# One image moved from the preparation into the first batch, the scan of the expert weights spread out, the router and the first feed-forward tokens rearranged

## The reference, cut to what matters

```python
# x: (4, 256, 48, 48) float32
x = x + conv(_ln_c(x))              # LayerNorm over the 256 channels at each pixel, then:
#   k    = relu(conv7x7_dilation2(ln, w1) + b1)            256 -> 128 channels
#   attn = softmax(relu(batchnorm(conv1x1(k, w2) + b2)))   49 weights for each pixel
#   out  = sum over the 49 taps p of shift_p(ln) * attn[p]
t = tokens(x)                       # (4, 2304, 256)
t = t + ffn(_ln_t(t))
#   logits = mean over an image's tokens @ Wr + br;  softmax, capacity scale, softmax, top 2 of 8 experts
#   h = gelu(xf @ W1[e] + b1[e]);  y = h @ W2[e] + b2[e];  weighted sum of the two experts
#   LayerNorm(out + x) * gamma + beta
```

## Time and profile before

| what | value |
|---|---|
| time of 3 runs: lowest, median, highest | 972.19, 973.37, 975.27 us |
| the profiled execution's own time | 967.95 us |
| its span, first to last instruction | 966.2 us |
| PE busy | 905.5 us, 94% |
| DVE, ACT, POOL busy | 698.6, 528.8, 143.4 us |

### The profile page before, as it was taken

One profiled execution on the slowest core, in us unless ns is written; L12 is line 12 of the kernel. 1 busy time (PEld: TensorE's weight loads), 2 busy tenths in 40 slices (PEclk: granted clock), 3 DMA queues, 4 the chain that ended last, 5 costly groups with the idle time before them and its releaser, 6 DMA issues. The chain is left out here.

```text
span 966.2 us, 19549 instructions
## 1 busy us (share of the span) xinstructions
PE 905.5 (94%) x7659; PEld 752.6 (78%) x7659; DVE 698.6 (72%) x1825; ACT 528.8 (55%) x981; POOL 143.4 (15%) x164
## 2 busy tenths in 40 slices
PE   2887999999999999899999948999999999999997
PEld 2776888888888888798999935777777777777776
DVE  4798566477658649745779867778877887788767
ACT  4797343443345221034445629677776878687751
POOL 1100010000010100200123220212121121212122
PEclk9899999999999999899999969999999999999999
DMA  9721311123200154620568663543364245423211
GB/s 220 206 73 50 99 50 51 51 75 79 64 26 26 40 164 123 193 50 2 148 170 224 152 165 77 142 105 66 85 162 100 51 99 154 93 64 85 67 34 50
DMA packets 134826, 95.01 MB, mean 98 GB/s; under 512 B 63579, under 2 KB 129516, under 8 KB 134636
## 3 DMA queue, kind: packets, MB, share of 16 engines
q1 hardware_dynamic: 134734, 93.77, 38.0%
HBM read 54.91 MB, written 29.40 MB: 87 GB/s over the span
## 5 line engine op out<-in xcount | busy, mean ns | idle before, releaser
L1335 PE MATMUL pM<-V,U 128*128 128x264 f16 (+3 forms) x2352 | 291.3, 281 | 0.0
L1335 PEld LDWEIGHTS pM<-V,U 128*128 128x128 f16 x2352 | 228.9, 98 | 43.1
L1876 ACT ACTIVATE gf<-pH,b1c,sc 128x384 f32<-128x384 f32 x192 | 127.7, 669 | 82.8 <-issue 67.2
L2169 PE MATMUL pH<-V,w1h 128*128 128x384 f16 x768 | 157.7, 328 | 4.4 <-ACT gf L1876 2.4
L2183 PE MATMUL pY<-w2h,gh 128*128 128x256 f16 x576 | 157.0, 273 | 0.3 <-DVE w2l L2028 0.3
L2183 PE MATMUL pY<-w2h,gl 128*128 128x256 f16 x576 | 157.0, 273 | 0.0
L2183 PE MATMUL pY<-w2l,gh 128*128 128x256 f16 x576 | 157.0, 273 | 0.0
L2036 DVE SCALAR_TENSOR_TENSOR gl<-gf,sc,gh 128x384 f16<-128x384 f32 x192 | 112.1, 620 | 48.9 <-ACT gh L1867 48.9
L2169 PEld LDWEIGHTS pH<-V,w1h 128*128 128x128 f16 x768 | 74.9, 98 | 54.1 <-ACT gf L1876 4.8
L1867 ACT ACTIVATE gh<-gf,sc 128x384 f16<-128x384 f32 x192 | 115.5, 616 | 0.0
L789 ACT CAST V<-pV 128x336 f16<-128x336 f32 x96 | 42.0, 437 | 132.1 <-PE pV L1306 132.1
(11 more groups left out here) (253 smaller groups left out, 1357.5 us busy)
## 6 DMA issues: line engine op xcount, KB each, us to landing
xa<-in_xt SPq DMA_DIRECT2D x16, 576.0 KB, 6.5
xs_scratch<-xs SPq DMA_DIRECT2D x16, 576.0 KB, 4.3
V<-t_scratch SPq DMA_DIRECT2D x24, 384.0 KB, 3.8
out<-o SPq DMA_DIRECT2D x23, 384.0 KB, 2.9
xs<-in_ew SPq DMA_DIRECT2D x16, 512.0 KB, 4.4
U<-xs_scratch SPq DMA_DIRECT2D x16, 480.0 KB, 4.7
V<-in_w1g SPq DMA_DIRECT2D x6, 784.0 KB, 8.8
w1r<-in_ew SPq DMA_DIRECT2D x8, 512.0 KB, 4.1
```

The source lines that it names most:

```text
L1335: return nc.tensor.matmul(out[:, :, first:end], U[:, k, hi_u, piece, :], V[:, b % 2, hi_v, k, c, :, first + TILES * d:end + TILES * d], st ...
L1876: nc.scalar.activation(gf[:, (JB * m + j) % GBUFS, :], pH[:, (JB * m + j) % HBUFS, 0:CN], ACT.Gelu, bias=b1c[:, j // FB, j % FB:j % FB + 1 ...
L2169: last = nc.tensor.matmul(pH[:, (JB * m + j) % HBUFS, 0:CN], w[:, k, c, f * P:(f + 1) * P], xT[:, s, x, c, :], start=(i == 0), stop=(i == ...
```

## The change

Five edits, each with its core in the diff.

- The preparation ends with image 3 in place of image 4. The first batch prepares five images (4 to 8), with tables of its own, and its `turn_v` run at points 2 to 13 in place of 0 to 11 (`TURNS_FROM`). At the start `tap_scale(0)` stands behind the first two of the six `bn_stats` of `ln(0)` in place of behind all of it.
- `UNITS_SLOT` spreads the 17 units over ten points.
- `BY_PE` becomes images 14 and 15: image 15 is summed by `sum_tokens`, `accumulate(15)` is gone, and `accumulate(13)` moves ahead of `statistics(14)`. `take_low` and `turn` of the two early chunks move behind the loop.
- The router: the factor 1/2304 goes into the router's weights ahead of the loop, one operation of the capacity scale goes, the constants `ones` and `mhalf3` are set in the first block, each weight load is issued as soon as its own expert's number is read, and ACT normalises and splits chunk 2 ahead of the first `gelus`, not behind.
- `HBUFS` goes from 3 to 5; two unused banks are given up for it.

```diff
-LN_SLOT = {0: 1, 3: 2, 6: 3, 10: 4}
-SPLIT_SLOT = {2: 1, 5: 2, 8: 3, 13: 4}
+LN_SLOT = [{0: 0, 2: 1, 5: 2, 8: 3, 11: 4}] + [{0: 1, 3: 2, 6: 3, 10: 4}] * (B - 1)
+NORM_SLOT = [{0: 0, 3: 1, 6: 2, 9: 3, 12: 4}] + [{1: 1, 4: 2, 7: 3, 11: 4}] * (B - 1)
+SPLIT_SLOT = [{1: 0, 4: 1, 7: 2, 10: 3, 13: 4}] + [{2: 1, 5: 2, 8: 3, 13: 4}] * (B - 1)
+TURNS_FROM = [2] + [0] * (B - 1)
...
-STAGES, UNITS_SLOT = 3, {1: 1, 2: 2, 3: 2, 4: 2, 5: 2, 6: 2, 7: 3, 8: 3}
+STAGES, UNITS_SLOT = 3, {1: 1, 2: 2, 3: 2, 4: 2, 5: 2, 6: 2, 7: 2, 8: 1, 9: 1, 10: 2}
...
-ADDED, BY_PE = 1, IMGS - 2
+ADDED, BY_PE = 1, (IMGS - 2, IMGS - 1)
...
-                if n - CHUNKS_AT - 2 in range(EARLY_CHUNKS):
-                    tokens.turn(sp, 0, n - CHUNKS_AT - 2)
+            tokens.turn(sp, 0, 0)
             store_stats(B - 1)
+            tokens.turn(sp, 0, 1)
...
             spread_mags(0)
-            ln(0)
+            ln_stats(0, third(0))
             tap_scale(0)
+            ln(0, range(NT // 3, NT))
             ln(1)
...
-                    m = V_TURNS * BI * (b + 1) + 2 * k
-                    turns = b < B - 1 and k < V_SLOTS
+                    m = V_TURNS * BI * (b + 1) + 2 * (k - TURNS_FROM[b])
+                    turns = b < B - 1 and 0 <= k - TURNS_FROM[b] < V_SLOTS
...
+            nc.vector.tensor_scalar(wrs[:, :, :], wrs[:, :, :], 1.0 / SB, None, ALU.mult).then_inc(wr_scaled, 1)
             for n in range(IMGS):
                 if 1 <= n <= BI:
                     normalise(B - 1, n - 1)
+                if n == IMGS - 2:
+                    accumulate(n - 1)
                 statistics(n)
...
-                if ADDED * BI < n < IMGS - 1:
+                if ADDED * BI < n < IMGS - 2:
                     accumulate(n - 1)
-                if n - CHUNKS_AT - 2 in range(EARLY_CHUNKS):
-                    tokens.take_low(dve, 0, n - CHUNKS_AT - 2)
-            accumulate(IMGS - 1)
+            for m in range(EARLY_CHUNKS):
+                tokens.take_low(dve, 0, m)
             take_stats(B - 1)
...
-            nc.vector.tensor_scalar(mean[:, :], mean[:, :], 1.0 / SB, None, ALU.mult).then_inc(mean_step, 1)
...
-            sum_tokens(BY_PE)
+            sum_tokens(BY_PE[0])
+            sum_added(B - 1)
             turn_stats(B - 1)
-            sum_added(B - 1)
+            sum_tokens(BY_PE[1])
             sum_shifts(B - 1)
...
-HBUFS, GBUFS = 3, JB
+HBUFS, GBUFS = 5, JB
...
-            nc.gpsimd.memset(ones[:, :], 1.0).then_inc(c_set, 1)
-            nc.gpsimd.memset(mhalf[:, :], -0.5).then_inc(c_set, 1)
-            pool.wait_ge(c_set, 2)
...
+            normalise(0, EARLY_CHUNKS)
             nc.scalar.activation(rc[:, 7:8], rc[:, 4:5], ACT.Gelu)
             split_w1(0)
+            take_x(0, EARLY_CHUNKS)
             act.wait_ge(bias_step, 1)
             gelus(0, 0)
-            normalise(0, 2)
-            take_x(0, 2)
...
-            do(nc.vector.tensor_scalar(r[:, 5, :], pY[0:B, 1, 0:EXPERTS], float(SB), None, ALU.mult))
-            do(nc.vector.reciprocal(r[:, 5, :], r[:, 5, :]))
-            do(nc.vector.tensor_scalar(r[:, 5, :], r[:, 5, :], CAPACITY, 1.0, ALU.mult, ALU.min))
+            do(nc.vector.reciprocal(r[:, 5, :], pY[0:B, 1, 0:EXPERTS]))
+            do(nc.vector.tensor_scalar(r[:, 5, :], r[:, 5, :], CAPACITY / SB, 1.0, ALU.mult, ALU.min))
```

More of the change, by code:

```diff
@@ L879, in _ @@
                         magnitude(2 * (pair + 1) + MAGS_THEN.index(j))
-                    if j in NORM_PARTS:
+                    if j in NORM_PARTS and pair + 1 < BI:
                         normalise_x(pair + 1, third(NORM_PARTS[j]))
-                    if j == XHI_AT:
+                    if j == XHI_AT and pair + 1 < BI:
                         x_high(pair + 1)
@@ L904, in _ @@
                         copy_sum(b)
-                    if LN_SLOT.get(k - 1) is not None and BI * (b + 1) + LN_SLOT[k - 1] < IMGS:
-                        normalise_x(BI * (b + 1) + LN_SLOT[k - 1])
+                    if k in NORM_SLOT[b] and BI * (b + 1) + NORM_SLOT[b][k] < IMGS:
+                        normalise_x(BI * (b + 1) + NORM_SLOT[b][k])
                     if turns:
@@ L1190, in _ @@
                         v_low(V_TURNS * pair + j - V_LATE)
-                    if j in LN_PARTS and pair + 2 <= BI:
+                    if j in LN_PARTS and pair + 2 < BI:
                         if LN_PARTS[j] < 2:
@@ L1204, in _ @@
                         bn_scales()
-                x_low(pair + 1)
+                if pair + 1 < BI:
+                    x_low(pair + 1)
             for b in range(B):
                 for k in range(NP):
-                    m = V_TURNS * BI * (b + 1) + 2 * k
-                    turns = b < B - 1 and k < V_SLOTS
+                    m = V_TURNS * BI * (b + 1) + 2 * (k - TURNS_FROM[b])
+                    turns = b < B - 1 and 0 <= k - TURNS_FROM[b] < V_SLOTS
                     if turns:
                         v_low(m)
-                    if k in SPLIT_SLOT and BI * (b + 1) + SPLIT_SLOT[k] < IMGS:
-                        x_low(BI * (b + 1) + SPLIT_SLOT[k])
+                    if k in SPLIT_SLOT[b] and BI * (b + 1) + SPLIT_SLOT[b][k] < IMGS:
+                        x_low(BI * (b + 1) + SPLIT_SLOT[b][k])
                     if 0 < b < B - 1 and MAPS_AT < k <= MAPS_AT + BI:
@@ L1241, in _ @@
                         normalise(b - 1, 0, BI)
-                    if LN_SLOT.get(k) is not None and BI * (b + 1) + LN_SLOT[k] < IMGS:
-                        ln(BI * (b + 1) + LN_SLOT[k])
+                    if k in LN_SLOT[b] and BI * (b + 1) + LN_SLOT[b][k] < IMGS:
+                        ln(BI * (b + 1) + LN_SLOT[b][k])
                     if turns:
@@ L1502, in _ @@
                     for c in range(CC):
-                        if b < B - 1 and k < V_SLOTS:
-                            turn_v(V_TURNS * BI * (b + 1) + 2 * k + c)
+                        if b < B - 1 and 0 <= k - TURNS_FROM[b] < V_SLOTS:
+                            turn_v(V_TURNS * BI * (b + 1) + 2 * (k - TURNS_FROM[b]) + c)
                         conv(b, k, c)
@@ L1569 @@
 JB = TOPK * FB
-R_STEPS, IDX_STEP = 22, 11
+R_STEPS, IDX_STEP = 21, 10
 TBUFS = CHUNKS
@@ L1642, in turn, with ffn_phase @@
                                self.xs2[:, s].rearrange("p a c t x -> p (a c t x)")).then_inc(self.x_turned[s], 16)
-def ffn_phase(nc, mean, wsum, consts, tokens, ew1, eb1, ew2, eb2, gamma, beta, out):
+def ffn_phase(nc, mean, wsum, consts, ones, mhalf, tokens, ew1, eb1, ew2, eb2, gamma, beta, out):
     ident, wrs, brs = consts
```

46 lines of the change are left out of this document (23 added, 23 removed).

## The result

| | median | runs | lowest to highest | ratio to the kernel before (95%) |
|---|---|---|---|---|
| before | 973.20 us | 4 | 972.19 to 975.27 | |
| after | 965.01 us | 4 | 964.42 to 966.74 | 0.9911 (0.9896 to 0.9927) |

The changed kernel is 0.9% faster, 8.2 us by the medians, against a forecast of 964.2 us. The two *profiled* executions lie only 1.2 us apart (967.95 and 966.74 us). That of before is a lucky one, 5.2 us under its median here, and that of the changed kernel lies 1.7 us above its own: over the 74 timed runs of before that list a clock the times go from 966.36 to 977.12 us, with a median of 972.09. What makes them differ is told under the first experiment.

What follows compares the result with a forecast made beforehand. PE, busy nine tenths or more of nearly every slice, bounds the kernel, so only its idle stretches count. 0.3 - 5.5 - 2.2 - 1.8 = -9.2 us gives a 964.2 us median, range 959.5 to 969.5.

Steps and rivals of the forecast that it cites:

- Part 1: Preparation and first batch: early scale's cost, missing fifth image's saving and crowded points nearly cancel, +0.3 us, between -3 and +3.
- that just fits: First batch, point 2: image 4 is ready at 107.5 us, PE gets there at 107.7.
- Rival 2: Preparation: the early scale costs nothing and no low clock follows; first part becomes -3, 961 us; chance 0.15.
- rival 6: First batch: DVE's list too full for five images, 18 us lost, 982 us; chance 0.04.
- Part 2: Units, last batch: point 9's 3.16 us wait and 2.45 us of lower clock go; -5.5 us, bounds -3.2 and -7.
- Rival 4: Last batch: units don't free point 9, or the clock stays low; -1 to -2.5, 967 to 969 us; chance 0.13.
- Part 3: End of attention and router: shorter chain to the router's first matmul, -2.2 us, bounds 0 and -3.5.
- Part 4: First chunks: chunk 2's earlier place on ACT gains -1.8 us, bounds -0.5 and -2.4; five banks worth nothing.
- The lock: End of attention: image 15's power on POOL waits for DVE's second `take_low`; 2.9 us dearer, 967 us; chance 0.12.
- theory A: Whole kernel, set for the experiments: the forecast's parts add up as priced.
- theory B: Whole kernel, set for the experiments: most of the gain is the clock.
- Theory C: Start of the kernel, set for the experiments: the early scale costs its 1.8 us to the end.

Runs made afterwards that it cites:

- the first experiment: The kernel before, unchanged, profiled and timed once more: median 971.90 us, ratio 1.0017.
- the late scale: The changed kernel with `tap_scale(0)` behind the whole of `ln(0)` again: median 961.22 us, ratio 0.9889; a second time 962.93 us, ratio 0.9906.
- The kernel with the units alone: The kernel before with the units at the new points and nothing else: median 965.54 us, ratio 0.9942.
- The last run: The late scale with image 15 added by DVE's `accumulate`, placed with `take_stats` between the two `take_low`: median 961.69 us, ratio 0.9882.
- the kernel with the old order: The changed kernel, five banks kept, with chunk 2's `normalise` and `take_high` behind the first `gelus` on ACT again: median 966.07 us, ratio 0.9922.

## Why the prediction was right, point by point

**Part 1, forecast +0.3: +0.4 at the start of the second batch.** The terms went as told: `turn_v(0)` at 26.44 (told: near 26.6), the first convolution at 96.92 (96.5), the wait on `v_low` at point 9 of 0.85 (1.0). Two went otherwise in this profile, and they are one: "I let the first convolution run at the lower level" came out 1.4 us better, PE was at point 2 before image 4, and so "that just fits" missed by 1.01 us. In the three profiles where the lower level did come, image 4 fits, as forecast. The +0.4 owes something to luck all the same. The five profiles with the late scale start the second batch at 177.8 us in the mean, so the missing fifth image gains 2.0 us against the old preparation's 179.8, and the early scale costs 2.4. The forecast had 1.5 and 1.8; both are too small, and the errors cancel. Rival 2 (the early scale costs nothing) is refuted in the traces. In rival 6's sum of DVE's work five long `y_points` should be six, 3.5 us more; nothing hangs on it.

**Part 2, forecast -5.5: -5.6 us** (2.2 either way). That the wait goes is shown, 2.0 to 3.2 us in the three profiles that have it. Of the rest the forecast had the right size and too simple a cause; that the total meets it to 0.1 us is luck. It took the lower clock for what the wait leaves behind, one convolution at 2.45 us. The kernel with the units alone has one such convolution elsewhere, and the profile of the changed kernel four without any wait ahead of them, the first at point 9: "the low clock still there at point 9", one of the forecast's own signs of being wrong, was there. In the mean of the runs the lower level is rarer with the new units (0.972 against 0.968), not gone; why, no run shows. The changed kernel's ten runs have a mean of 0.970 only, 1.9 us by the line in place of 3.2. Rival 4's half "the clock stays low" is thus what the profiled execution showed, and not what the runs show on average.

**Part 3, forecast -2.2: -0.4 us.** `statistics(15)` ends 6.50 us behind the start of `attend(15)` and not 7.37: the 0.9 of the forecast. `sum_tokens(14)` starts 4.63 us behind it and not 6.34, since the power of image 14 takes 1.17 us where the earlier trace rows has 4.04; the forecast didn't count that. The step that failed is "`sum_tokens(15)`, 2.50 us as image 14's": behind `sum_tokens(14)` and `sum_added` it runs at a granted clock of 0.50 and takes 4.26 or 4.28 us in eight of the nine profiles that have it, and 3.90 in one. These 1.8 us eat the 1.2 us counted for the exchange with `accumulate` and `sum_added`, and more. The sign "some 2 us nearer to the end of `attend(15)`" didn't come: the mean over the nine is 14.75 us to the router against 14.92. From there to the first `layer1` it is 9.57 to 9.68 against 9.91 to 9.95 (10.35 in the ninth profile, which reads both experts first). The last run shows what was to be had: 13.83.

**Part 4, forecast -1.8: -1.9 to -2.7 us** from the first `layer1` to the end of the span (386.71 and 385.87 us in two profiles of the changed kernel, 388.57 in before), and 1.8 us at an equal clock in the kernel with the old order. "Five banks are worth nothing there" was wrong by 0.75 us: PE's full slices hid six short waits of its weight loads. The signs of this part came: no wait in the second `layer1`, 0.81 us ahead of the first `layer2`.

**The lock.** POOL's power of image 15 ran beside `take_low` and took 1.41 us, and 1.17 where DVE was idle beside it; the multiplication behind it took 0.36 and not 0.20. So 0.4 us went there, and 2.9 was the rival's price. The Trainium skill, "SBUF — State Buffer", "Who interferes with whom", says that such instructions exclude each other for a whole instruction. That agrees with 0.24 and 0.16 us, each less than one of the four `take_low` instructions (1.96 us together). What failed here is what I drew from it, that the power "waits until the second `take_low` is done": it ended 0.4 us ahead of that. But this isn't so everywhere. The power of image 14 takes 4.04 us in each of the three profiles with the old end of attention, and in the earlier trace rows it ends at 558.76 us, 1.0 us behind the end of the chain that DVE began beside it (`accumulate(13)` and a `take_low`, to 557.73), as if it had waited for all of it. Why one power is held by a whole chain and another by part of one instruction stays open. Timeline of before, DVE:

```profile
554.74 2.05 DVE L1110 SCALAR_TENSOR_TENSOR U<-xs,U 120x256 f32<-120x256 f32 x5
556.72 1.01 DVE L1634 SCALAR_TENSOR_TENSOR V<-V 128x384 f16<-128x384 f32 x2
```

The sum: +0.4 - 5.6 - 0.4 - 2.3 = -7.9 us, measured -8.2. Part 2 is from timed runs and uncertain by 2.2 us, the others are from traces, so that they close to 0.3 us is partly luck. Against the forecast of -9.2, part 3 gave 1.8 us less and part 4 some 0.5 more. So theory A holds but for part 3. By the line the changed kernel gains 6.2 us at an equal clock and 1.9 by the clock, so theory B doesn't hold. Theory C is shown to the second batch, not to the end.

What stays open: why the clock falls in the last batch at all. Four profiles with the new units have one slow convolution there, seven have three or four, among them two profiles of the same kernel (the late scale: 49.70 and 53.16 us for the stage). No run took the `spread` matmuls away to see. Nor do the timed runs settle whether the late scale gains the 2.4 us that its traces show at the second batch.

## What to carry to other kernels

When single executions scatter by 1%, set the time of every run against its mean granted clock before comparing two profiles: a lucky profile of before and an unlucky one of the changed kernel hid seven of the eight microseconds here. Price a matmul that moves behind short ones at the clock that rows at that place show, not at that of the same matmul elsewhere. And where two engines meet at a barrier, a shorter chain on one gains only if the DMA issues of the other, with the instructions that release them, move up too.

## What the runs showed of the hardware

The granted clock falls with PE busy without a gap. Windows of the changed kernel, the second batch and the last:

```profile
180.00:270.00 90.00, 90.00 (x867) 78.89 (x865) 61.35 (x177) 39.47 (x77) 8.92 (x19) 1.00 0.25 67
356.00:455.00 99.00, 97.83 (x854) 84.67 (x852) 68.78 (x139) 23.63 (x47) 7.58 (x6) 0.93 0.38 105
```

PE has no gap in the first, and in the second none but the 1.2 us at its very end, ahead of attention. In the last batch the short `spread` matmuls, 8 of 48 or 60 columns at a time, stand between the convolutions; there the clock is 0.93, it falls and rises between neighbouring rows, and execution by execution at other points. That the short matmuls are the reason is not shown. The forecast had a fall only behind a wait.
